# The divisor of the second attention: one product with a constant matrix and a reciprocal of the whole block, scaled on GpSimd

## The reference

```python
logits = jnp.einsum('bhqd,bhkd->bhqk', q, k) * scale
attn = jax.nn.softmax(logits, axis=-1)
y = jnp.einsum('bhqk,bhkd->bhqd', attn, v)
y = y.transpose(0, 2, 1, 3).reshape(B, T, D)
return y @ wo_w + wo_b
```

## Time and profile before

| | |
|---|---|
| median of 3 executions | 4111.77 us (4111.37 to 4117.78) |
| profiled execution, its own time | 4113.93 us |
| its span, first to last instruction | 4112.1 us |
| mean granted TensorE clock | 0.984 |
| PE busy | 3803.7 us, 92% of the span |
| DVE busy | 2600.6 us, 63% |
| ACT busy | 2378.7 us, 58% |
| POOL busy | 1927.9 us, 47% |

### The profile page before, as it was taken

One profiled execution on the slowest core, in us unless ns is written; L12 is line 12 of the kernel. 1 busy time (PEld: TensorE's weight loads), 2 busy tenths in 40 slices (PEclk: granted clock), 3 DMA queues, 4 the chain that ended last, 5 costly groups with the idle time before them and its releaser, 6 DMA issues.

```text
span 4112.1 us, 65455 instructions
## 1 busy us (share of the span) xinstructions
PE 3803.7 (92%) x23682; PEld 2697.8 (66%) x23682; DVE 2600.6 (63%) x4143; ACT 2378.7 (58%) x4593; POOL 1927.9 (47%) x1219
## 2 busy tenths in 40 slices
PE   6999999999999999999999878999999999999987
PEld 4777777777777777777777654555555555555544
DVE  5665666666566666656656656666666666666662
ACT  3565655556565555655656535666666666666654
POOL 2554455555445455544545543444444444444412
PEclk9999999999999999999999978999999999999998
DMA  4444344344344334444434423232222222322220
GB/s 112 93 103 97 84 103 103 80 101 103 88 93 103 92 88 103 95 96 93 99 92 93 112 49 50 51 55 53 52 53 53 54 52 54 55 54 50 50 42 16
DMA packets 152368, 315.59 MB, mean 77 GB/s; under 512 B 23088, under 2 KB 76720, under 8 KB 152048
## 3 DMA queue, kind: packets, MB, share of 16 engines
q1 hardware_dynamic: 152048, 311.39, 35.3%
HBM read 33.43 MB, written 25.17 MB: 14 GB/s over the span
## 4 chain that ended last, share of the span: by engine, by line
PE 55%; DVE 20%; ACT 13%; issue 7%; POOL 3%; DMA 0%; SPq 0%; DVEq 0%; POOLq 0%; ACTq 0%
PE ps_o L656 10%; DVE neg_max L987 7%; ACT e_a L815 5%; PE ps_o L728 5%; PE ps_t L222 4%; DVE max_b L1128 4%; PE ps_t L764 4%; PE ps_s L701 3%; ACT raw_a L837 3%; PE ps_t L687 3%; PE ps_t L229 3%; PE ps_t L755 3%; PE ps_t L640 3%; PE ps_m L222 2%; DVE xn L1106 2%
## 5 line engine op out<-in xcount | busy, mean ns | idle before, releaser
L535 POOL TENSOR_TENSOR e_a<-e_a,recip 128x1024 f32<-128x1024 f32 x512 | 969.5, 1894 | 1045.1 <-DVE recip L994 1045.1
L815 ACT ACTIVATE e_a<-ps_s,neg_max 128x512 f32<-128x512 f32 x1024 | 693.9, 684 | 249.6 <-DVE neg_max L987 238.7
L853 ACT ACTIVATE et<-ps_s 128x1024 f32<-128x1024 f32 x512 | 523.6, 1023 | 432.9 <-PE ps_s L715 432.8
L1128 DVE TENSOR_REDUCE max_b<-ps_s 128x2 f32<-128x1024 f32 x512 | 623.9, 1219 | 209.3 <-PE ps_s L701 208.0
L987 DVE TENSOR_REDUCE neg_max<-ps_s 128x2 f32<-128x1024 f32 x512 | 621.1, 1213 | 25.3 <-PE ps_s L628 25.3
L656 PE MATMUL ps_o<-et_a,v_a 128*64 128x256 f32 x4096 | 470.3, 382 | 0.0
L640 PE MATMUL ps_t<-ident,e_a 128*128 128x128 f32 x2736 | 394.6, 275 | 41.9 <-DVE et_a L1001 35.8
L627 PE MATMUL ps_s<-stack_a 128*128 128x512 f32 x1024 | 413.0, 403 | 12.9 <-DMA stack_a<-raw_a 8.6
L569 POOL TENSOR_TENSOR h_lo<-h,h_hi 128x512 fp32r<-128x512 f32 x256 | 329.2, 1300 | 180.0 <-ACT h_hi L897 180.0
L628 PE MATMUL ps_s<-stack_a 128*128 128x512 f32 x1024 | 402.4, 393 | 0.0
L640 PEld LDWEIGHTS ps_t<-ident,e_a 128*128 128x128 f32 x2736 | 321.2, 141 | 110.7 <-DVE et_a L1001 51.8
(11 more groups left out here) (207 smaller groups left out, 7965.1 us busy)
## 6 DMA issues: line engine op xcount, KB each, us to landing
stack_a<-raw_a SPq DMA_DIRECT2D x256, 384.0 KB, 4.7
stack_a<-raw_a SPq DMA_DIRECT2D x256, 256.0 KB, 4.3
stack_a<-raw_a SPq DMA_DIRECT2D x256, 128.0 KB, 3.6
q_stack<-roped_q SPq DMA_DIRECT2D x256, 64.0 KB
k_stack<-roped_k SPq DMA_DIRECT2D x256, 64.0 KB
x_a<-X SPq DMA_DIRECT2D x16, 512.0 KB, 3.5
X<-x_a SPq DMA_DIRECT2D x16, 512.0 KB, 3.0
x_ahead<-X SPq DMA_DIRECT2D x16, 512.0 KB, 3.8
```

The source lines that it names most:

```text
L535: nc.gpsimd.tensor_tensor(e_a[:, u % 4, :, :], e_a[:, u % 4, :, :], factor, ALU.mult).then_inc(e_normed, 1)
L815: ins = nc.scalar.activation(e_a[:, u % 4, j, :], ps_s[:, 2 * (u % 2) + j, :], ACT.Exp, bias=neg_max[:, u % 4, j:j + 1], accum_out=sums[:, ...
L853: nc.scalar.activation(et[:, v % 5, :, :], ps_s[:, 2:4, :], ACT.Exp)\
L1128: nc.vector.reduce_max(max_b[:, u // 4 % 2, :, u % 4], ps_s[:, score_bank(u):score_bank(u) + 2, :], AX.X, negate=True).then_inc(max_done, 1)
```

## The change

"sum" becomes one product: a constant matrix `spread` (128 by 128; column m has a one in row 16 of m's band) times `weighted` puts each head's sum into all 32 rows of its band, for all 512 queries. DVE takes the reciprocal of that whole bank, 128 rows by 512, into `recip_wide`. POOL multiplies `weighted` by it into `heads_b` (`scale_heads`, one step later in POOL's order). The "recip" product, `widen` and DVE's multiplication go. `recip_wide` has one buffer, so a reciprocal waits for POOL's multiplication of the quad before.

```diff
-            plan += [(16 * g + 45.5, "recip", "attn", g, s) for g in range(QUADS)]
...
+                def scale_heads(i, s, fill):
+                    wait_emptied(pool, fill)
+                    if s and i == 0:
+                        wait_filled(pool, fill_of["wo", "ffn1", TB - 1, s - 1])
+                    nc.gpsimd.tensor_tensor(heads_b[:, i, :], weighted[:, i % 2, :], recip_wide[:, :], ALU.mult).then_inc(scaled, 1)
...
+                        for kind, part, i, s, fill in steps_of.get(step - 2, []):
+                            if kind == "sum":
+                                scale_heads(i, s, fill)
...
-                            for g in range(QUADS):
-                                wait_emptied(pe, fill_of["recip", "attn", g, s])
+                            pe.wait_ge(scaled, QUADS * (s + 1))
...
-                        for t in range(TB):
-                            last = nc.tensor.transpose(bank(fill)[:, t * P:(t + 1) * P], weighted[:, i % 2, t * P:(t + 1) * P],
-                                                       ident[:, :])
...
+                        last = mm(bank(fill), spread[:, :], weighted[:, i % 2, :], start=True, stop=True)
...
-                        wait_emptied(act, fill_of["recip", "attn", (n - 2) % QUADS, (n - 2) // QUADS])
+                        act.wait_ge(scaled, n - 1)
...
+                    picked = ident[:, :].rearrange("p (h w) -> p h w", w=32)[:, :, HB:HB + 1].to_broadcast([P, 4, 32])
+                    nc.vector.tensor_copy(spread[:, :].rearrange("p (h w) -> p h w", w=32), picked)
...
                     elif kind == "sum":
                         wait_filled(dve, fill)
-                        sums = bank(fill).rearrange("p (t h w) -> p t h w", h=4, w=32)[:, :, :, HB]
-                        emptied(nc.vector.reciprocal(recip_b[:, i % 2, :, :], sums), fill)
-                    elif kind == "recip":
-                        wait_filled(dve, fill)
-                        emptied(nc.vector.tensor_tensor(heads_b[:, i, :], weighted[:, i % 2, :], bank(fill), ALU.mult), fill)
+                        if s or i:
+                            dve.wait_ge(scaled, QUADS * s + i)
+                        emptied(nc.vector.reciprocal(recip_wide[:, :], bank(fill)), fill)
```

More of the change, by code:

```diff
@@ L120, in hybrid_block_kernel @@
         max_b = at("max_b", 1.375, [P, 2, 2, TB])
-        recip_b = at("recip_b", 1.5, [P, 2, TB, 4])
-        recip_wide = at("recip_wide", 204, [P, TB, 4, 32])
+        spread = at("spread", 1.5, [P, P])
+        recip_wide = at("recip_wide", 204, [P, S])
         w1_raw = at("w1_raw", 154, [P, KT, FF])
@@ L185, in hybrid_block_kernel @@
         res_ready = sem("res_ready")
-        widened = sem("widened")
         st_done = sem("st_done")
@@ L189, in hybrid_block_kernel @@
         copied = sem("copied")
+        scaled = sem("scaled")
         m_high = sem("m_high")
@@ L773, in product @@
                                                    ident[:, :])
-                    elif kind == "sum":
+                    else:
                         pe.wait_ge(copied, QUADS * s + i + 1)
-                        for t in range(TB):
-                            last = nc.tensor.transpose(bank(fill)[:, t * P:(t + 1) * P], weighted[:, i % 2, t * P:(t + 1) * P],
-                                                       ident[:, :])
[L779 to L783, removed]
+                        last = mm(bank(fill), spread[:, :], weighted[:, i % 2, :], start=True, stop=True)
                     if kind not in ("wo", "down", "v") or i % 2 == 1:
@@ L897, in hidden_high @@
                     nc.scalar.activation(h_hi[:, i, :], h32[:, n % 4, :], ACT.Copy).then_inc(hi_copied, 1)
[L899 to L904, removed]
                 def parts_high(i, half, s):
@@ L939, in _ @@
                                 hidden_high(part, i, s, fill)
-                        for kind, part, i, s, fill in steps_of.get(step - 3, []):
-                            if kind == "sum":
-                                widen(i, s, fill)
                         for s in range(BATCH):
```

## The result

The changed kernel takes 4239.0 us (median of four runs, 4234.6 to 4239.6), the kernel before 4111.6 us: a ratio of 1.0304, with a 95% interval of 1.0291 to 1.0316. It is slower by 127 us; the forecast was 4250, with a range of 4180 to 4340. The profiled execution of the changed kernel took 4239.58 us, with a span of 4237.8 us.

A forecast was written before the change was run, and what follows sets the result against it. The prediction took PE's work and its waits for DVE's maxima as the bound. To the profiled 4113.9 us it added 101 for 16 samples and 37 for the clock: 4252, so 4250 us against the median, range 4180 to 4340.

The forecast's parts named there:

- What bounds the kernel: Second stage: a sample is as long as PE's work and waits; scores wait 68.1 us for DVE's maxima.
- The price of the reciprocal: DVE's new reciprocal of 512 elements a row out of PSUM takes 3.48 us, from the slope between two shorter reciprocals.
- The forecast's other estimate: Upper bound for the reciprocal: with a fixed 0.13 us taken off, 8 ns an element, 4.2 us.
- The stalls: Scores behind the four quads' reciprocals wait 1.23, 1.04, 2.00 and 1.56 us, 5.83 us a sample.
- the formula: Stall of the next scores is the reciprocal's length less 0.44 us, less the maxima's time to spare in that quad.
- the second rival: PE's other waits in a sample, 4.8 us, swallow most of the loss: 4136 us; chance 0.10.
- Product and transposes: On PE, the new f32 product costs 0.37 us more a quad; the dropped transposes back save 0.53 us a quad.
- the first rival: DVE's reciprocal runs like other operations, 0.68 us, so no quad stalls and PE sheds 10 us: 4102 us; chance 0.10.
- The rotation: POOL's fourth scaling delays the rotation, then ACT's rounding and exponentials, which the turned scores need: +1.1 us a sample.
- The clock: PE's clock falls one and a half times a sample behind the new stalls, 1.54 us each: 37 us.
- The ends: The two ends of the second stage differ a little both ways from its bulk; left in the range.
- The sum: Stalls, product, transposes and rotation make 6.3 us a sample, 101 us over 16; with the clock, 4250 us.

The follow-up runs named there:

- experiment 1: Changed kernel with VectorE's reciprocal of the block replaced by a copy of the same 512 columns, all else kept: 4122.1 us, ratio 1.0020.
- experiment 4: Kernel before plus one unused reciprocal of 64 rows by 512 columns ahead of the old reciprocal: 4231.4 us, ratio 1.0289.
- Experiment 7: Kernel before plus two unused 128x512 products on GpSimd behind the keys' last rotation, from the second sample on: 4126.6 us, ratio 1.0036.
- experiment 3: Changed kernel with GpSimd's scaling three steps later in its order, reciprocal whole: 4209.0 us, ratio 1.0236.
- experiment 8: Changed kernel with rounded weighted values and constant matrix, reciprocal cut at column 352, each piece behind a maximum, fourth quad scaled on VectorE: 4123.1 us, ratio 1.0025.

## Why the prediction was right

**What bounds the kernel** held. PE's time and PE's waits for the maxima make the sample, and the loss sits where the forecast put it: 4.99 of 7.08 us in the pairs behind a reciprocal. Experiments 1 and 4 show it from both sides: without the long reciprocal 117 us go, and with nothing but it 118 come.

**The price of the reciprocal**, the step that decided everything, was 3.48 us and is 3.36. The extrapolation over the elements held from 16 to 512: pieces of 160, 256 and 352 columns took 1.14, 1.75 and 2.35 us, and from 256 to 512 columns it is 6.3 ns each. The rule of the Trainium skill ("Vector Engine (DVE) Microarchitecture Reference", § 5.2 Measured stream behaviour on trn2) that gives 1.04 ns a column for built-in operations of one source does not hold for it. The copy of the same block in experiment 1, 0.61 us from its start to that of the maxima, follows it. The forecast's other estimate, 8.3 ns an element, is too high by a third.

**The stalls** were 5.83 us a sample and are 4.7 us of idle PE. With R = 3.36 the formula gives 5.35; the other 0.6 is that the maxima start 0.08 us ahead of the reciprocal's listed end and take 1.16 us there, not 1.23. Then PE catches up: behind the stalls it sheds 0.89 us a sample more than the transposes explain (2.64 without the fall's 1.52, less 1.75), as it does in experiment 4 (0.93). That is the second rival, at a fifth of its size. Net the stalls cost 4.1 us a sample. This term was over-sized by 1.7.

**Product and transposes** were +1.48 and -2.12 and are +1.77 and -1.75. The product's price came from half of eight instructions that follow each other; from its start to the scores it takes 1.02 us (3203.48 to 3204.50). PE's saving, 10 us in the sum and in the first rival, does not exist.

**The rotation** was near in size, 1.1 against 1.44 us, and wrong in mechanism, so the size was luck. The step that failed is the last one: "The turned scores at 3096.02 need them". ScalarE does wait for POOL's late rotation, by the list of waits of the changed kernel (2500 to 4100 us; us in all, times, longest; in the kernel before it is 2.9 us, 13 times):

```profile
ACT roped_k L912 <- POOL k_rot L587: 39.1, 28, 2.5
```

But what PE waits for ahead of the turned scores (L723 by itself, whole stage; us, times) is ScalarE for 7.0 us in eight places, and in the kernel before it was 5.3 us, also in eight:

```profile
  ACT et L853: 7.0, 8
```

What is late is DVE. Its instructions, POOL's beside them and PE's scores behind the fourth quad, in the kernel before and then in the changed one:

```profile
3086.40 1.19 DVE L1124 TENSOR_TENSOR roped_q<-q_rot,roped_q 128x512 fp32r<-128x512 f32 x1
3092.95 0.72 DVE L1106 TENSOR_SCALAR xn<-x_ahead,mean_var,rstd 128x256 f32<-128x256 f32 x2
...
3088.80 2.94 POOL L582 TENSOR_TENSOR k_rot<-k_rot 128x512 f32<-128x512 f32 x2
3093.75 2.36 POOL L563 TENSOR_TENSOR x_ahead<-x_ahead,b_rows 128x1024 f32<-128x1024 f32 x1 [2.01 <-DVE xn L1106]
...
3085.68 0.49 PE L701 MATMUL ps_s<-k_stack,q_stack 48*128 48x512 f32 x2
3088.78 0.49 PE L701 MATMUL ps_s<-k_stack,q_stack 48*128 48x512 f32 x2 [0.62 <-DVE max_b L1128]
3093.09 0.50 PE L701 MATMUL ps_s<-k_stack,q_stack 48*128 48x512 f32 x2 [0.66 <-DVE max_b L1128]
3095.68 0.50 PE L701 MATMUL ps_s<-k_stack,q_stack 48*128 48x512 f32 x2
3099.14 0.50 PE L701 MATMUL ps_s<-k_stack,q_stack 48*128 48x512 f32 x2 [0.71 <-DVE max_b L1128]
```

```profile
3134.08 1.67 DVE L1116 TENSOR_TENSOR roped_q<-q_rot,roped_q 128x512 fp32r<-128x512 f32 x1
3141.11 1.69 DVE L1098 TENSOR_SCALAR xn<-x_ahead,mean_var,rstd 128x256 f32<-128x256 f32 x2
...
3133.92 1.29 POOL L583 TENSOR_TENSOR k_rot<-k_flat,cos 128x512 f32<-128x512 f32 x1
3139.98 2.67 POOL L587 TENSOR_TENSOR k_rot<-k_rot 128x512 f32<-128x512 f32 x2
...
3133.36 0.50 PE L709 MATMUL ps_s<-k_stack,q_stack 48*128 48x512 f32 x2
3136.94 0.51 PE L709 MATMUL ps_s<-k_stack,q_stack 48*128 48x512 f32 x2 [1.10 <-DVE max_b L1120]
3141.24 0.51 PE L709 MATMUL ps_s<-k_stack,q_stack 48*128 48x512 f32 x2 [0.63 <-DVE max_b L1120]
3144.18 0.50 PE L709 MATMUL ps_s<-k_stack,q_stack 48*128 48x512 f32 x2 [0.27 <-DVE max_b L1120]
3148.27 0.51 PE L709 MATMUL ps_s<-k_stack,q_stack 48*128 48x512 f32 x2 [0.95 <-DVE max_b L1120]
```

`roped_q` is 0.48 us longer and the pair behind it 0.49; the two blocks of `xn` are 0.97 us longer and the two pairs behind them 0.96. The instructions are the same; POOL's rotation, which the fourth scaling delays, now runs beside them. In the kernel before, POOL stands idle while the two blocks run. The rows also show what the longer instructions wait for: `roped_q` ends at 3135.75, 0.54 us behind POOL's product that had begun before it (3135.21), and the blocks of `xn` end at 3142.80, 0.15 us behind POOL's pair (3142.65). From 2600 to 3900 us all twelve long `roped_q` of the changed kernel end 0.55 us behind an instruction of POOL, to 0.01 us. Experiment 7 makes the 0.96 in the kernel before, without any delay of ScalarE, and experiments 3 and 8 take it away with the rotation back in time. The 0.49 of `roped_q` moves with that instruction's length in the same way: 1.80 us and +0.61 in experiment 1, 1.36 and +0.18 in experiment 3, where POOL stood elsewhere. No run tried it alone.

**The clock** was 1.5 falls a sample and is one, always behind the longest of the four stalls; and I had set it against none before, where it is one in four samples. A fall costs 1.52 us, by the third quad's pair with and without one (+0.55 here, -0.97 in experiment 3); the forecast had 1.54. At one a sample against one in four samples that is 16 falls against four over the stage: 12 more, 18 us, not 37.

**The ends** were left to the range and hold 14 us. The first scores of the stage come 3.3 us later than in the kernel before, which I have not explained; in the experiments that figure lies between -0.5 and +3.9. From the last scores to the end it takes 10.6 us more. The chain that ended last shows one part of that (start, us, what):

```profile
4187.75 3.37 DVE recip_wide L1146
...
4191.18 1.27 POOL heads_b L569
...
4192.59 5.55 PE ps_t L752 x16
```

From the last sums' product to the output projection it is 5.98 us, and 3.23 from the transposes on in the kernel before; the projection then starts at half the clock and takes 9.0 us in place of 7.2. The other 6 us lie ahead of this and were not followed further.

**The sum** per sample is 4.1 + 1.77 - 1.75 + 1.44 = 5.56 us in place of 6.3. Over 16 samples that is 89, with 18 for the clock and 14 at the ends 121, against the 126 by which the spans differ. The last sample, 9.4 us longer where a usual one is 7.1, holds about half of what is left. That the forecast's 138 is so near is in part luck: over-sized stalls and falls stood against the saving that does not exist and the ends left out. On the other side, the first rival (fast reciprocal) fell with the 3.36 us, and even its prize: experiment 1 has a fast instruction in that place and is not faster than before.

## What to carry to other kernels

Price a new instruction by the nearest rows of the same operation, over their slope, and not by other operations of its engine; then put its length against the time that the work queued behind it has to spare at each place. A product that replaces transposes saves nothing while its own time is that of the transposes. When one engine's work moves in time, look at what the other engines then run beside it: here GpSimd's work in another place alone, without any wait of ScalarE behind it, made VectorE's instructions longer and cost 1 us a sample.

## What was unexpected in the hardware

- A reciprocal on VectorE takes 6.3 ns a column out of PSUM: 128x512 in 3.36 us, 128x256 in 1.75, and 64x512, half the partitions, also in 3.36.
- Some of VectorE's instructions wait for an instruction of GpSimd that began before them. A 128x512 subtraction (`roped_q`) takes 0.68 us when nothing holds it up and 1.67 when it has to wait, and then ends 0.55 us behind GpSimd's product; of two 128x256 blocks of `xn` the second took 1.37 us in place of 0.40. It goes the other way too: in the kernel before, two products of GpSimd take 2.94 us behind a `roped_q` that began 0.16 us ahead of them (3088.64) and took 0.68, where two alike take 2.51 in experiment 3. The reciprocal out of PSUM does not vary (3349 to 3360 ns).
- The same stall of 1.74 us at the same place of the program was followed by half the clock eleven times out of twelve between 2600 and 3900 us in the changed kernel, and four times out of twelve in experiment 3.
